# Recurrent layer: VectorE's gate product placed in front of the second scans

## The reference

```python
r = (xr @ Wr.T); k = (xk @ Wk.T); v = (xv @ Wv.T)
g = jax.nn.silu(xg @ Wg.T)
def step(s, rkvw):
    r_t, k_t, v_t, w_t = rkvw
    a = k_t[..., :, None] * v_t[..., None, :]
    out = jnp.einsum('bhi,bhij->bhj', r_t, u * a + s)
    s = a + w_t[..., :, None] * s
    return (s, out)
_, out = jax.lax.scan(step, s0, rkvw)
...
og = ((og - m) / jnp.sqrt(va + 1e-05)).reshape(b, l, e) * gn_w + gn_b
x1 = x + og * g @ Wo.T
...
rr = jax.nn.sigmoid(xr2 @ Wfr.T)
kk = jnp.square(jax.nn.relu(xk2 @ Wfk.T))
return x1 + rr * (kk @ Wfv.T)
```

## Time and profile before

| | us |
|---|---|
| median of 3 runs | 1021.28 (1017.84 to 1023.32) |
| the profiled execution, its own time | 1015.32 |
| span of the profiled execution | 1013.5 |
| PE busy | 953.1 (94%) |
| DVE busy | 593.0 (59%) |
| ACT busy | 450.9 (44%) |
| POOL busy | 408.1 (40%) |

### The profile page before, as it was taken

One profiled execution on the slowest core, in us unless ns is written; L12 is line 12 of the kernel. 1 busy time (PEld: TensorE's weight loads), 2 busy tenths in 40 slices (PEclk: granted clock), 3 DMA queues, 4 the chain that ended last, 5 costly groups with the idle time before them and its releaser, 6 DMA issues.

```text
span 1013.5 us, 21546 instructions
## 1 busy us (share of the span) xinstructions
PE 953.1 (94%) x8337; PEld 800.2 (79%) x8337; DVE 593.0 (59%) x972; ACT 450.9 (44%) x990; POOL 408.1 (40%) x572
## 2 busy tenths in 40 slices
PE   6999998888999999999999999999998998999986
PEld 4777777776788888899888988888997877677854
DVE  5999993668544433344364444333448447999961
ACT  3566764138633333333343333333333243676553
POOL 2243354975365243333166433433315623243330
PEclk9999999999999999999999999999999999999989
DMA  8100000220011111111102111101100100000000
GB/s 294 31 2 2 2 1 22 89 97 1 1 54 53 47 52 32 40 36 52 48 6 69 38 52 47 52 27 46 36 22 12 43 11 1 2 1 12 7 11 16
DMA packets 24147, 37.15 MB, mean 37 GB/s; under 512 B 4432, under 2 KB 16528, under 8 KB 23824
## 3 DMA queue, kind: packets, MB, share of 16 engines
q1 hardware_dynamic: 24080, 36.23, 11.5%
HBM read 35.17 MB, written 1.05 MB: 36 GB/s over the span
## 4 chain that ended last, share of the span: by engine, by line
PE 71%; DVE 14%; POOL 5%; issue 5%; ACT 5%; DMA 0%; SPq 0%; DVEq 0%; ACTq 0%; POOLq 0%
PE ps L1209 17%; PE ps L731 11%; PE ps L1226 9%; PE ps L1268 6%; PE ps L1862 6%; PE ps L1244 3%; PE ps L820 3%; DVE sb L608 2%; PE ps L1254 2%; DVE sb L602 2%; DVE sb L2292 2%; PE ps L2015 1%; ACT sb L1649 1%; PE ps L1940 1%; PE ps L243 1%
## 5 line engine op out<-in xcount | busy, mean ns | idle before, releaser
L781 POOL TENSOR_TENSOR sb<-sb 128x256 fp32r<-128x256 f32 (+1 forms) x128 | 98.4, 769 | 299.1 <-DMA sb<-in_heads_a 149.5
L1209 PE MATMUL ps<-sb 128*128 128x512 f32 x768 | 187.7, 396 | 1.0 <-issue 1.0
L1209 PEld LDWEIGHTS ps<-sb 128*128 128x128 f32 x768 | 139.7, 188 | 32.8 <-ACT sb L1342 3.2
L731 PE MATMUL ps<-sb 128*128 128x256 f32 x1152 | 147.2, 286 | 0.0
L731 PEld LDWEIGHTS ps<-sb 128*128 128x128 f32 x1152 | 141.0, 192 | 1.8
L783 POOL TENSOR_TENSOR sb<-sb 128x256 fp32r<-128x256 f32 (+1 forms) x128 | 115.0, 898 | 10.0
L1439 DVE SCALAR_TENSOR_TENSOR sb<-ps,sb 128x512 fp32r<-128x512 f32 x64 | 45.1, 747 | 96.1 <-ACT sb L1375 96.0
L1226 PE MATMUL ps<-sb 128*128 128x256 f32 x768 | 99.2, 286 | 0.4 <-DVE sb L1407 0.4
L1226 PEld LDWEIGHTS ps<-sb 128*128 128x128 f32 x768 | 95.0, 191 | 3.0 <-issue 0.9
L1419 DVE TENSOR_REDUCE sb<-ps 128x8 f32<-128x520 f32 x32 | 22.4, 700 | 126.6 <-PE ps L1244 126.6
L1342 ACT ACTIVATE sb<-ps,sb 128x512 f32<-128x512 f32 x64 | 43.8, 684 | 107.9 <-PE ps L1209 107.8
(11 more groups left out here) (215 smaller groups left out, 1638.0 us busy)
## 6 DMA issues: line engine op xcount, KB each, us to landing
sb<-in_heads_a SPq DMA_DIRECT2D x32, 386.0 KB, 3.1
sb<-in_heads_c SPq DMA_DIRECT2D x16, 256.0 KB, 3.5
sb<-in_heads_b SPq DMA_DIRECT2D x32, 128.0 KB, 3.0
sb<-in_mlp_a SPq DMA_DIRECT2D x16, 128.5 KB, 2.1
sb<-in_mlp_b SPq DMA_DIRECT2D x16, 128.0 KB, 2.1
sb<-in_w_r SPq DMA_DIRECT2D x1, 2048.0 KB, 7.4
sb<-in_encT SPq DMA_DIRECT2D x1, 1024.0 KB, 6.4
sb<-in_ctx SPq DMA_DIRECT2D x1, 1024.0 KB, 7.7
```

What stands on the lines that cost most here:

```text
L731: last = pe.matmul(m.acc(t), lhsT[x], rhs[w], start=opens and n == 0, stop=False, skip_group_check=True)
L781: pool.tensor_tensor(high, src, one, ALU.mult).then_inc(*G.did(name + "_high", u))
L1209: last = pe.matmul(m.ps[u][:, c, :], m.w_parts[u][w][:, (KD * q + k) * P:(KD * q + k + 1) * P], rows[x][:, k, c * 512:(c + 1) * 512], star ...
```

## The change

One call moves in VectorE's loop. `gate(slot - 4)` leaves its place behind `receive(slot - 5)` and stands in front of `scan1(slot - 5)`. No instruction is added or removed, the waits of each step stay the same, and no other engine's order changes.

```diff
@@ -2379,13 +2379,13 @@
         scan0(slot - 5)
         group_rstd(slot - 6)
         group_norm(slot - 6)
+        gate(slot - 4)
         scan1(slot - 5)
         ffn(slot - 8)
         if slot == 3:
             vec.wait_ge(*ph.pe.at("fc2", 1, MLP_ROUNDS - 1))
             add_half(vec, m, 1)
         receive(slot - 5)
-        gate(slot - 4)
         attended(slot - 6)
         close(slot - 8)
         mix1(slot - 3)
```

## The result

The changed kernel takes 1043.6 us (median of 4 runs, 1039.65 to 1044.9), the kernel before on the same chip 1020.25 us (1017.84 to 1023.32). The ratio is 1.0245, with a 95% interval of 1.0202 to 1.0289. It is slower by 23.4 us.

A forecast was written before the change was run, and what follows sets the result against it. TensorE was taken to bound slots 8 to 10, VectorE slots 5 to 7. A new loop's +18.0 us and clock falls' +8.2 made +26.2 on a median of 1021.3, so 1047.5 us, range 1036 to 1059.

The forecast's parts named there:

- The wait in front of L2266: VectorE's gate product waits for ScalarE's copy: 3.7 us in slots 6 and 7, 4.95 or more in 8 to 11.
- The scans, 3.3 us: VectorE's five second scans, moved away from GpSimd's receptance product, take 3.3 us for 4.11 (slot 10) and 5.17 (slot 6).
- Slot 5, -1.0: VectorE's slot 5: scans end 1.1 us later, less 0.3, and the 1.81 us hole takes this up; net -1.0.
- Slots 6 and 7, +2.8 at x1: VectorE's wait less cheaper scans makes +1.9 in each slot; x1 of slot 7 comes 2.8 us later.
- more: Rival: scans stay at 4.11 us, each clock fall costs 2.66, further falls would add; +34, 1055.5 us; chance 0.13.
- Slot 8, +5.7 at turn_ffn: TensorE's gather starts 1.9 us late, then turn_ffn waits for VectorE's ffn and starts 5.7 us late.
- the +18.0: Sum of the recurrent layer's terms at unchanged clock: 5.7 (slot 8), 7.6 (slots 9, 10), 4.7 (slot 11).
- The loop, 22.55 us a slot and 22.2 in slot 11: Closed path over TensorE, ScalarE and VectorE: 22.55 us for 18.75 in slots 9 and 10, 22.2 for 17.52 in 11.
- The clock, 2.05 us for each of four falls: TensorE falls to half clock after its new pauses in slots 8 to 11: +8.2 us, bounds 0 and 10.6.
- VectorE absorbs the wait: Rival: TensorE runs ahead, the wait shrinks to 2.04 us, only slots 6 and 7 pay; +2.8, 1024 us; chance 0.07.
- Faster: Rival: TensorE's 3.0 us gate waits and 1.9 us in each of slots 6 and 7 come back; -6.8, 1014.5 us; chance 0.03.
- The loop without the clock: Rival: TensorE stays at full clock after its pauses; +18.0, 1039.3 us; chance 0.17.

The follow-up runs named there:

- e1: The changed kernel run again unedited, beside the kernel before on the same chip: 1052.1 us against 1015.8, ratio 1.035.
- e10: Changed kernel with ScalarE's tanh and copy in front of its heads step and three gate buffers for two: ratio 1.0226 to the kernel before.
- e7: Kernel before with the gate product moved in front of the second scans in slot 5 alone: ratio 1.0014 to the kernel before.
- e4: Changed kernel with 12 unused matmuls in TensorE's pause before turn_ffn, beside VectorE's slots 8 to 11: ratio 1.0183 to the kernel before.
- e3: Changed kernel with ScalarE's tanh and copy in front of its heads step: ratio 1.0283 to the kernel before.
- e5: Kernel before with the gate product moved in front of the second scans in slots 8 to 11 alone: ratio 1.0249 to the kernel before.
- e2: Changed kernel with VectorE's ffn step moved in front of the gate product: ratio 1.0137 to the kernel before.
- e9: Changed kernel with VectorE's ffn step in front of the gate product up to slot 11 only: ratio 1.0168 to the kernel before.

## Why the prediction was right

The direction and the mechanism held. The size held in the first timing: +23.4 us measured, +26.2 forecast, range 1036 to 1059 for 1043.6. The second timing (e1) has +36.4 us, 10 more than forecast, with 1052.1 still in the range, so how large the loss is between 23 and 36 us stays open. In the profiled pair it is +28.5 us of span, of which 27.8 in this layer; with e1's profile it is 32.0 in the layer. Step by step, against the profiled pair:

- **The wait in front of L2266.** Laid out as 3.7 us in slot 6 and 4.95 or more in slots 8 to 11; measured 3.83 in slots 6 and 7, 5.04 to 5.64 in slots 8 to 11.
- **The scans, 3.3 us.** Measured 3.24, down from 4.15 and 5.17. That GpSimd's products were what had made them long fits e10, where two of them fall on the scans again and these take 3.97.
- **Slot 5, -1.0.** Measured -1.2, and alone in e7 -1.3 up to slot 6.
- **Slots 6 and 7, +2.8 at x1.** Measured +3.4. The difference is VectorE's wait of 0.76 us for L1970, which ran at half clock in slot 7. TensorE's pauses for x1 were 2.4 and 1.2 us, with a stretch at half clock at both. I had named a fall there in the case "more" and left it out of the sum.
- **Slot 8, +5.7 at turn_ffn.** Measured +7.7, the largest miss of a term in the +18.0: +2.5 at gather for 1.9 laid out, another 1.5 from gather to turn_heads, which ran at half clock and for which nothing was laid out, and 3.7 for 3.8 from there to turn_ffn.
- **The loop, 22.55 us a slot and 22.2 in slot 11.** With the clock held by e4 it is 22.4 and 22.05.
- **The clock, 2.05 us for each of four falls.** The distances to slots 9, 10 and 11 are some 1.6 us above e4's, so each of these three falls cost less than I took. Behind the fourth pause B is 3.6 us longer than before, with 15 us at half clock for 7; if all of this goes to the fourth fall, it cost more. The four together came to some 8.4 us, for 8.2 forecast, but that is luck of the sum, since no single term fits, and B was 7.8 us longer than before in e1. Every pause of TensorE of 3.6 us or more in slots 8 to 11, 17 of them in five profiles (the changed kernel, e1, e3, e5 and e10), had a fall in it or behind it. This agrees with what the forecast cites from the Trainium skill, page "TensorE: Matmul & The Clock Gate", section "HAM oscillation — how this bites in real kernels".

The rivals: "VectorE absorbs the wait" falls with the profile of the changed kernel, where the wait is 5 us and not 2 and slots 8 to 11 cost most of the loss. The opposite, that the wait costs wherever it stands, falls with e2, since a wait of 3.9 us is left there and the loss in A is down by three quarters. "Faster" had its one true part in slot 5. "The loop without the clock" is what e4 shows between slots 8 and 11, and is not what the changed kernel does.

Against the first timing the forecast of the change is 2.8 us high, against the profiled pair 1.6 us low in the layer, and against the second timing 10.2 us low. That the sum came so close to the first is in part luck: 2 us too little up to slot 8 and 0.5 too much in the loop stand beside a spread of several us from the clock.

## What to carry to other kernels

Before a step is moved forward on an engine, look at when its last input is ready on the other engines, and then at what the step is put in front of: a wait on an engine with time to spare costs if what another engine waits for now stands behind it, since a path over three engines then becomes a loop of every slot (here 22.4 us for 18.75 at full clock). Moving only as far as the inputs allow (here between ffn and receive, not in front of the second scans) avoided the loss; its gain of 2.5 us in the profiles is not shown in the timed runs. Add up the new loop link by link from the trace; here that gave its length to 0.2 us.

## What was not expected of the hardware

The stretches at half clock had very different lengths. The windows shown, which lie about or just inside them, are 2.9 and 6.5 us long before, and 3.2, 10.2, 10.3 and 13.3 us in the runs after. In two profiles (e7 and e9) the clock stayed at half for 10.2 us although TensorE was busy for all of it. In e7 the last wait of TensorE in front of it was one of 1.1 us, shorter than the 2.1 us pause after which the clock had stayed full in the kernel before. So the pause in front doesn't tell by itself what a fall will cost. What sets the length was not tried.
